# Sparse experts on one core: gathers one pair further ahead, tokens transposed behind the gate and up products

## The reference, cut to what matters

```
x = x + mamba_block(ctx_1024, gate=layernorm(x))          # [4, 512, 512], a scan of 16 states
h = layernorm(x)                                          # 2048 tokens of 512
scores = softmax(h @ gate_w.T)                            # 64 experts
w, i = top_k(scores, 6)
buf[e, slot] = h[token]                                   # at most 64 tokens of each expert, zeros where fewer
y = (silu(buf @ w_gate[e]) * (buf @ w_up[e])) @ w_down[e] # 512 -> 352 -> 512, for each expert
x = x + sum over the kept experts of w * y + (silu(h @ sw_gate) * (h @ sw_up)) @ sw_down
```

## Time and profile before

| | |
|---|---|
| median of 3 runs | 1169.33 us (1167.05 to 1171.11) |
| the profiled execution | 1168.47 us |
| its span | 1166.7 us |
| mean granted clock of TensorE | 0.857 of full speed |
| TensorE busy | 922.5 us, 79% |
| VectorE, ScalarE, GpSimd busy | 590.3, 477.9, 590.1 us |
| DMA, mean over the span | 215 GB/s, 250.50 MB |

### The profile page before, as it was taken

The page is one execution under the profiler, slowest core; times in us unless marked ns, Lnnn a source line. Parts: engine busy times, 40 slices in busy tenths (PEclk is TensorE's granted clock), DMA queues, the critical chain, the costliest instruction groups (busy, mean ns, idle before and its releaser), DMA issues.

```text
span 1166.7 us, 12225 instructions
## 1 busy us (share of the span) xinstructions
PE 922.5 (79%) x4049; PEld 502.5 (43%) x4049; DVE 590.3 (51%) x833; ACT 477.9 (41%) x853; POOL 590.1 (51%) x334
## 2 busy tenths in 40 slices
PE   5446636567889767889769995899999899997966
PEld 2144335454344454344455445444444443443432
DVE  2087977959657859667859754321212112111111
ACT  3556653765572765472765512322121212111111
POOL 0498799966497856487857650112121211122211
PEclk9568765668989857999969996899999999998988
DMA  9332434432322533323433628399999999999992
GB/s 322 110 126 73 145 110 145 145 120 83 111 86 95 178 134 108 110 78 104 144 114 137 226 99 318 146 340 394 395 401 390 400 399 391 392 390 401 384 318 28
DMA packets 68361, 250.50 MB, mean 215 GB/s; under 512 B 10522, under 2 KB 13094, under 8 KB 68044
## 3 DMA queue, kind: packets, MB, share of 16 engines
q1 hardware_dynamic: 56332, 226.14, 51.2%
q0 software_dynamic: 7744, 18.88, 6.6%
q10 hardware_dynamic: 4224, 4.72, 1.2%
HBM read 230.54 MB, written 19.17 MB: 214 GB/s over the span
## 4 chain that ended last, share of the span: by engine, by line
PE 45%; DMA 15%; DVE 13%; ACT 9%; issue 9%; POOL 8%; SPq 1%; POOLq 0%; DVEq 0%; ACTq 0%
PE ps L697 10%; PE ps L567 9%; PE ps L734 9%; DMA out_rows<-xn,idxs 5%; DMA arena<-xn_rows,idu 5%; PE ps L758 4%; POOL arena L1342 3%; PE ps L710 3%; DVE ps L1106 3%; DVE arena L1106 3%; DMA arena<-bc_rows 3%; DVE arena L1113 2%; POOL arena L1347 2%; PE ps L778 2%; ACT ps L919 2%
## 5 line engine op out<-in xcount | busy, mean ns | idle before, releaser
L567 PE MATMUL ps<-ident,arena 128*128 128x128 f32 (+2 forms) x1408 | 252.6, 336 | 153.2 <-POOL arena L1347 91.5
L567 PEld LDWEIGHTS ps<-ident,arena 128*128 128x128 f32 (+2 forms) x1408 | 215.8, 186 | 257.6 <-POOL arena L1347 105.3
L1342 POOL TENSOR_TENSOR arena<-arena 128x1024 f32<-128x1024 f32 x128 | 299.7, 2355 | 27.4 <-PE ps L567 15.0
L919 ACT ACTIVATE ps<-arena,An 128x511 f32<-128x511 f32 x256 | 165.8, 680 | 195.1 <-DVE ps L1114 150.9
L1106 DVE TENSOR_TENSOR_SCAN ps<-ps,arena 128x1024 f32<-128x1024 f32 x76 | 174.0, 2289 | 48.9 <-ACT ps L919 36.5
L1366 POOL DMA_INDIRECT out_rows<-xn,idxs x32 | 50.9, 1592 | 279.1 <-ACT xn L818 151.5
L1347 POOL TENSOR_TENSOR arena<-arena 128x1024 f32<-128x1024 f32 x52 | 122.3, 2352 | 117.1 <-DVE arena L1106 117.1
L697 PE MATMUL ps<-xnT,sw 128*128 128x512 f32 (+1 forms) x328 | 160.2, 629 | 8.7 <-ACT hs L818 8.7
L734 PE MATMUL ps<-arena 128*64 128x352 f32 x968 | 165.8, 480 | 0.0
L1106 DVE TENSOR_TENSOR_SCAN arena<-ps,arena 128x1024 f32<-128x1024 f32 x52 | 118.9, 2286 | 31.7 <-POOL arena L1342 29.0
L1246 DVE TENSOR_TENSOR arena<-arena,ps 128x352 f32<-128x352 f32 x32 | 16.7, 521 | 208.0 <-PE ps L734 208.0
(11 more groups left out here) (150 smaller groups left out, 936.4 us busy)
## 6 DMA issues: line engine op xcount, KB each, us to landing
arena<-bc_rows SPq DMA_DIRECT2D x128, 512.0 KB, 4.6
arena<-in_L_ffn_w_down SPq DMA_DIRECT2D x60, 768.0 KB, 20.5
arena<-in_L_ffn_w_gate SPq DMA_DIRECT2D x61, 704.0 KB, 20.6
arena<-in_L_ffn_w_up SPq DMA_DIRECT2D x60, 704.0 KB, 18.1
arena<-in_x SPq DMA_DIRECT2D x4, 1024.0 KB, 6.8
xn_rows<-xn ACTq DMA_DIRECT2D x4, 1024.0 KB, 4.5
out_rows<-arena SPq DMA_DIRECT2D x4, 1024.0 KB, 4.9
extra<-in_L_ffn_w_up SPq DMA_DIRECT2D x4, 704.0 KB
```

Of the source, the lines that this page charges most:

```text
L567: return nc.tensor.matmul(dst, src, ident[0:k, 0:k], is_transpose=True, **kw)
L919: a = nc.scalar.activation(ps[:, 2 * (c % 2) + n, 1:L], dt[k][:, 1:L], ACT.Exp, scale=An[:, k, NB * g + n:NB * g + n + 1])
L1342: G.tensor_tensor(R[c % RING], dtu[k][:, None, :].to_broadcast([P, NB, L]), Brep[n % REPS], ALU.mult)\
```

## The change

On TensorE the transposition of the tokens of q + 1 stands behind the gate and up products of q instead of in front of them. On ScalarE the silu of q goes in front of the copy of the tokens of q + 1. On POOL four gathers instead of three are issued ahead of the loop, and turn q issues the gather of q + 4 instead of q + 3, still ahead of that turn's addition and scatter. Buffers, waits inside the functions, transfers and arithmetic are the same.

```diff
--- before.py
+++ after.py
@@ -792,9 +792,9 @@
                 claim(bank)
             tokens(0)
             for q in range(NPAIR):
+                gate_up_mm(q)
                 if q + 1 < NPAIR:
                     tokens(q + 1)
-                gate_up_mm(q)
                 if q == 0:
                     claim(6)
                     claim(7)
@@ -1058,9 +1058,9 @@
             act.wait_ge(s["xn_st"], 16 * B)
             evac_tokens(0)
             for q in range(NPAIR):
+                silu(q)
                 if q + 1 < NPAIR:
                     evac_tokens(q + 1)
-                silu(q)
                 evac_acts(q)
                 if q:
                     evac_merged(q - 1)
@@ -1379,11 +1379,11 @@
             pool.wait_ge(s["init_in"], 16 * 3)
             pool.wait_ge(s["yT_mm"], NQ)
             pool.wait_ge(s["out_st"], 16 * B)
-            for q in range(3):
+            for q in range(4):
                 gather(q)
             for q in range(NPAIR):
-                if q + 3 < NPAIR:
-                    gather(q + 3)
+                if q + 4 < NPAIR:
+                    gather(q + 4)
                 for n in items(q):
                     if ITEMS[n][0] == "down":
                         add_shared(n)
```

## The result

The changed kernel takes 1151.88 us (median of 4 runs, 1149.01 to 1153.42) against 1170.22 us for the kernel before on the same chips. The ratio is 0.984, with a 95% interval of 0.981 to 0.987. 1153 had been forecast, in a range of 1146 to 1161. The profiled execution has a span of 1147.3 us; 1150.2 was the sum. It is the shortest of the four: the other three have spans of 1149.5, 1150.8 and 1151.7 us.

What follows compares the result with a forecast made beforehand. Late gathers stall TensorE while weights stream at full DMA rate. With those waits gone, the weights' line ends at 1147.1 and the scatters' at 1150.2; the later plus 1.8 and 0.9 gives 1152.9, say 1153 us, range 1146 to 1161.

Steps and rivals of the forecast that it cites:

- the sum: Whole kernel: the later of the weights' end, 1147.1 us, and the scatters' end, 1150.2 us, decides the span.
- What bounds: Second stage: weights stream at full DMA rate, TensorE waits 24.9 us for gathers, 31.7 us lie behind the last weight.
- The gather's lead: POOL queue: short pairs leave a gather at least 14.7 us instead of 6.6, so all waits for gathers go.
- The held addition: POOL, turn 20: the shared addition is held some 3.4 us behind a gather that waits for weight columns.
- T + 10: POOL: a gather is issued about 10 us behind T, the start of its turn on TensorE.
- The line of scatters: POOL from scatter 19 at 994.4 us: steps of 9.9, with an addition 18.0; last scatter 1144.6, end 1150.2.
- The line of weights: End of kernel: last weight at 1135.4 us, then down product, merge, copy and last scatter, ending at 1147.1.
- It costs nothing there: TensorE: moving the 0.47 us token transposition behind the gate and up products adds no time.
- Waits for weights in the last third: TensorE: waits for weights were to appear in the last third of the pairs, as a sign of the forecast.
- the sum's start of the line of scatters: POOL: the scatter of pair 19 is issued at 994.4 us, its turn's start set by the weights' pace.
- Rival (B): POOL queue: gathers directly ahead make scatters land later; at 2 us more per step, 1190 us; chance 0.06.

Runs made afterwards that it cites:

- changed kernel's second execution: The changed kernel, unaltered, measured again on the same chip beside two other kernels; 1152.4 us, ratio 0.986 to the kernel before.
- light tail with the addition first: Changed kernel loading half of each gate and up matrix for pairs 29 to 31, shared addition ahead of its turn's gather; 1146.1 us.
- order only: Changed kernel's new order on TensorE and ScalarE, but gathers three ahead as in the kernel before; 1151.8 us, ratio 0.985.
- tokens behind the down product: Changed kernel with tokens of q+1 transposed behind the down product of q-1 instead of in front of it; 1153.0 us.
- that and addition first: Changed kernel with tokens transposed behind the down product and the shared addition moved ahead of its turn's gather; 1153.4 us.
- addition first again: Second measurement of the changed kernel with only the shared addition moved in front of its turn's gather on POOL; 1150.5 us.
- four index buffers: Changed kernel with four scatter index buffers instead of two, so VectorE's index step waits for the scatter four pairs back; 1153.1 us.
- no additions: Changed kernel without the four shared additions to the output on POOL, result wrong by that; 1147.0 us.
- gathers only again: Second measurement of only the change's POOL part, four gathers ahead, TensorE and ScalarE in the order of before; 1154.5 us.
- kernel with the gathers only: Only the change's POOL part, four gathers ahead, TensorE and ScalarE in the order of before; 1155.2 us in its first measurement.

## Why the prediction was right, and where it was not

- **What bounds: right.** The stream of weights is full and ends where it did (374 us behind the first silu, before and after), the waits for gathers were the fault, and all of the gain is in the stretch behind the last weight.
- **The gather's lead: right.** All waits for gathers went, as worked out. What the prediction didn't say is that each part alone does it: the order gives 4.9 us, the place on POOL 3.2 or more, and in short pairs some 2.3 us were missing (8.85 against 6.6). The place ahead of the scatter also makes the gather itself shorter, which was not in the sum: from issue to landing a median of 6.9 us in the changed kernel's second execution, against 8.8 before, where each was issued right behind a scatter (770 to 1130 us).
- **The held addition: right in kind, low in size.** It was put at 3.4 us; the addition goes 5.6 us later than when it stands first. The hold itself was right (the gather is issued 10.1 us behind the start of turn 21, T + 10 had been worked out), but turn 21 starts at 997.74 us and not at 994.5.
- **The line of scatters: right.** By the clock every issue from 19 to 29 is within 2.7 us of the sum, but an early first stage hides 1.7 us; behind the first silu they are up to 4.5 us later. The light tail with the addition first shows it as a line of its own. The end, 1147.3 against 1150.2, is earlier by those 1.7 us and because two unloaded steps stand at the end and not one: the scatter of 29 goes at 1130.00, when the stream is already thinning, and lands in 4.94 us; 5.8 from issue to issue where 9.9 was counted. So the total is nearer than its terms: late additions and an early end cancel, which is luck.
- **The line of weights: right to be there, too short and by another way.** In seven of the twelve experiments the chain of waits ends over it: order only, tokens behind the down product, that and addition first, addition first again, four index buffers, no additions, gathers only again. It goes over the down product of pair 30 and two scatters, and the end lies 12.6 to 15.4 us behind the last weight packet where 11.7 was counted; the longer ones hold the slow down product. That it put the last issue at 1141.5 us, and that it was 1141.57 us, is chance: the changed kernel ended over the scatters. That the two lines end close together was in the sum (1147.1 and 1150.2).
- **"It costs nothing there": wrong.** The moved transposition costs 0.21 us and the down product behind it 0.15, 0.36 in a short pair and some 9 us in all. The step took durations from the old order, where the transposition stood among full-width instructions. The total escaped because TensorE at 10.27 us a pair reaches pair 31 just when the weights do; at 9.91 it waits for them instead (11.7 us in the kernel with the gathers only).
- **"Waits for weights in the last third": wrong,** for that same term: one wait of 1.5 us. And the sum's start of the line of scatters (994.4, measured 993.85) was right by two errors that cancel: it took turn 20 as set by the weights, and TensorE's slower pace brought it to the same microsecond.
- **Rival (B), scatters slower behind a gather: no.** Most scatters are now issued 0.3 to 0.8 us behind a gather and land in 8.5 us (median), as before. Where one waits for the other, plain steps are 9.1 to 10.3 us, under the 11.35 at which it would have decided (in the second execution one is 11.2). The rule that stood with it, from the Trainium skill, DMA: Bandwidth & Descriptors, section "Queues, rings and completion order", is that each DMA engine takes turns between queues. That two transfers of one queue share a turn costs the scatters nothing visible here; the gathers, 6.9 us ahead of a scatter and 8.8 behind one, would fit it.

## What to carry to other kernels

When a stage is bound by a stream that is full anyway, look at what lies between the last byte and the end; that is all that a change can win, and two or three chains may end there together, so shortening one hands the end to the next. A transfer that is issued in a serial queue behind others needs its lead counted from when it is really issued; here 3 to 5 us of lead were enough, and a second source of lead brought nothing. Time won on an engine that then stands waiting for the stream is lost, and more with it: behind such a wait the product at the end took 4.4 to 5.4 us instead of 2.8. A wait put in front of a transfer holds everything behind it in that queue: place it behind what is on the chain that ends last.

## What the runs showed that had not been expected

- Transpositions between two groups of 64-column products cost TensorE more than their own time: four transpositions of 128 x 128 take 0.68 us between two groups of 64-column products, and the product behind them 0.15 us more, against 0.47 and nothing beside other full-width work (the chains of waits above; 0.36 us a pair).
- Waiting for the stream can cost TensorE its clock as well: behind waits for weights of 1.9 to 3.7 us the down product of pair 30 ran at a mean granted clock of 0.50 to 0.62 in seven executions and took 4.4 to 5.4 us. In three others, behind 1.5 to 2.0 us, it kept 1.00 and took 2.8.
- The same transposition in front of a merge that waits for VectorE makes a pair 0.26 us shorter than before (9.65 against 9.91).
- A scatter of 128 rows of 2 KB with addition mostly lands in 8.2 to 9.8 us while weights stream, whether a gather stands directly in front of it or not, and in 4.6 to 4.9 without them. In six executions one issued 10 to 13 us ahead of the last weight packet took 10.3 to 10.8.
- A gather of 128 rows beside the stream lands in 6.9 us (median) ahead of a scatter and in 8.8 directly behind one.
